# Where the scores' two waits stand among TensorE's column-strip sums in the attention stacks

## What is computed

```
for i in range(6):
    x = attn_layer(shift_tokens(x), Wqkv[i], q_scale[i], k_scale[i], Wo[i]) + x
    x = ffn_layer(shift_tokens(x), ln_g[i], ln_b[i], W1[i], b1[i], W2[i], b2[i]) + x

# attn_layer, 16 heads of 64, window 32
q, k, v = split(x @ Wqkv)
q = l2norm(q) * qs;  k = l2norm(k) * ksc
q, k = rotary(q), rotary(k)
out = softmax(mask(8 * q @ k.T)) @ v        # a query sees 64 keys: its window and the one before
return out @ Wo
```

## Time and profile before

| | us |
|---|---|
| median of three runs | 4347.09 |
| fastest and slowest of them | 4330.38, 4347.27 |
| the profiled execution | 4352.9 |
| its span, first to last instruction | 4351.2 |
| TensorE busy (matmuls) | 4027.8, 93% of the span |
| VectorE busy | 3345.6, 77% |
| ScalarE busy | 3100.0, 71% |
| GpSimd busy | 1798.7, 41% |

### The profile page before, as it was taken

The page is one execution under the profiler, slowest core; times in us unless marked ns, Lnnn a source line. Parts: engine busy times, 40 slices in busy tenths (PEclk is TensorE's granted clock), DMA queues, the critical chain, the costliest instruction groups (busy, mean ns, idle before and its releaser), DMA issues. The chain is left out here.

```text
span 4351.2 us, 113662 instructions
## 1 busy us (share of the span) xinstructions
PE 4027.8 (93%) x43857; PEld 2388.8 (55%) x43857; DVE 3345.6 (77%) x4981; ACT 3100.0 (71%) x7032; POOL 1798.7 (41%) x1071
## 2 busy tenths in 40 slices
PE   7997999999999999999967689999999999999998
PEld 3443555555555555555536545555555555555554
DVE  5774888888888888888735478888888888888885
ACT  3555777777777777777762267777777778777776
POOL 3111444444444444444404534444444444444442
PEclk7997999999999999999986589999999999999999
DMA  2212444444443443444300044444434444444342
GB/s 44 31 21 70 95 111 102 99 101 101 105 111 90 111 107 90 111 99 103 84 10 3 3 107 109 101 97 109 110 87 115 102 100 100 102 105 111 92 100 52
DMA packets 232520, 380.78 MB, mean 88 GB/s; under 512 B 59364, under 2 KB 122336, under 8 KB 231688
## 3 DMA queue, kind: packets, MB, share of 16 engines
q1 hardware_dynamic: 231560, 372.20, 36.9%
q10 hardware_dynamic: 384, 0.79, 0.1%
HBM read 39.22 MB, written 1.05 MB: 9 GB/s over the span
## 5 line engine op out<-in xcount | busy, mean ns | idle before, releaser
L835 POOL TENSOR_TENSOR b_prob<-b_prob,b_rinv 128x768 f32<-128x768 f32 x384 | 564.3, 1469 | 1778.3 <-DVE b_rinv L1281 1778.3
L841 POOL TENSOR_TENSOR b_prc<-b_prc,b_sws 128x1024 f32<-128x1024 f32 x384 | 907.7, 2364 | 72.2 <-DMA b_sws<-b_prs 72.2
L1143 ACT ACTIVATE b_prob<-ps,b_nmx 128x96 f32<-128x96 f32 x3072 | 749.0, 363 | 0.0
L885 PEld LDWEIGHTS ps<-ident,b_prob 128*128 128x128 f32 x3072 | 367.9, 140 | 406.5 <-ACT b_pT L1079 232.8
L1216 DVE SCALAR_TENSOR_TENSOR b_prc<-ps,b_qks,b_rot 128x512 f32<-128x512 f32 x768 | 571.1, 744 | 14.0 <-ACT b_sq L1104 13.3
L1218 DVE SCALAR_TENSOR_TENSOR b_prs<-ps,b_qks,b_rot 128x512 f32<-128x512 f32 x768 | 570.1, 742 | 0.0
L885 PE MATMUL ps<-ident,b_prob 128*128 128x128 f32 x3072 | 513.0, 281 | 46.5 <-DVE b_kr L1264 37.1
L1262 DVE TENSOR_TENSOR b_prc<-b_prc,ps 128x512 f32<-128x512 f32 x384 | 263.6, 686 | 369.9 <-PE ps L950 288.3
L1079 ACT ACTIVATE b_pT<-ps 128x512 f32<-128x512 f32 x724 | 435.5, 601 | 154.1 <-PE ps L885 151.1
L987 PE MATMUL ps<-b_wqkv,b_xs 128*128 128x256 f32 x1536 | 435.0, 406 | 2.2 <-DVE b_prs L1218 2.2
L938 PE MATMUL ps<-b_xs,b_wqkv 128*128 128x512 f32 x768 | 408.9, 614 | 23.3 <-issue 10.0
(11 more groups left out here) (293 smaller groups left out, 7218.0 us busy)
## 6 DMA issues: line engine op xcount, KB each, us to landing
b_sws<-b_prs SPq DMA_DIRECT2D x1536, 128.0 KB, 2.3
b_vs<-b_va SPq DMA_DIRECT2D x384, 256.0 KB, 3.8
b_wqkv<-in_L_ffn_Wqkv SPq DMA_DIRECT2D x96, 192.0 KB, 3.6
b_xs<-y SPq DMA_DIRECT2D x126, 128.0 KB, 2.3
b_wo<-in_L_ffn_Wo SPq DMA_DIRECT2D x96, 64.0 KB, 3.1
b_xs<-y SPq DMA_DIRECT2D x42, 127.8 KB, 2.4
b_rot<-in_rot SPq DMA_DIRECT2D x2, 2048.0 KB, 7.8
b_w<-in_L_ffn_W SPq DMA_DIRECT2D x24, 170.5 KB
```

The lines of the kernel that those rows point to most:

```text
L835: pool.tensor_tensor(prob[:, r, :, P - KEYS:P], prob[:, r, :, P - KEYS:P], rinv[:, r % 2, :].rearrange("p (b a) -> p b a", a=1).broadcast_ ...
L841: pool.tensor_tensor(prc[:, r, :, :], prc[:, r, :, :], sws[:, r % 2, :, :], ALU.add)\
L885: t = pe.transpose(bank[6][:, i * P:(i + 1) * P], prob[:, kd, 4 * e + 2 * h + m, :], ident[:, :])
L1143: g = act.activation(prob[:, kb, i, P - KEYS:P], wide[0][:, e * CH + m * KEYS:e * CH + (m + 1) * KEYS], ACT.Exp, bias=nmx[:, kb % 2, i:i + 1])
```

## The change

The function `strips` gets an argument `ahead`. Where it is set (and there is a unit b), `scores_ready` is called ahead of the fourth strip, inside the group. In odd slots in which the strips directly follow the second `turn` (all odd ones but those with `before == 5`), `turn` no longer gets b, so its last transposition waits for nothing of its own, and the call of `scores_ready` ahead of the masks, which only slots without a unit d had, falls away there. Even slots and the slots with `before == 5` keep their order. The number of matmuls and of waits stays the same, and nothing changes on the other engines.

```
-                def strips(U, b, pe=pe):
+                def strips(U, b, ahead, pe=pe):
                     pe.wait_ge(S["sqk_done"], ONE + U + 1)
                     if b:
                         pe.wait_ge(S["qn_done"], ONE + um(b)[0] + 1)
                     for s in range(4):
+                        if s == 3 and b and ahead:
+                            scores_ready(um(b)[0])
                         m = pe.matmul(bank[2][32 * s:32 * s + 32, :], head_of[:, :], sq[:, s, :],
                                       start=True, stop=True, skip_group_check=True)
                     m.then_inc(S["ss_mm"], 1)
@@
                     if d and before != 5:
-                        turn(UD, kd, 1, b)
+                        turn(UD, kd, 1, None if a and j % 2 else b)
                     if a and j % 2 and before != 5:
-                        strips(U, b)
+                        strips(U, b, True)
                     if b:
-                        if not d:
+                        if not d and not (a and j % 2):
                             scores_ready(UB)
                         mask(kb)
@@
                     if a and j % 2 and before == 5:
-                        strips(U, b)
+                        strips(U, b, False)
```

## The result

The changed kernel takes 4351.55 us (median of 20 runs, 4344.37 to 4371.22), the kernel before on the same chip 4343.36 (20 runs). One of the latter 20, of 5764.32 us, was a slow one and is left out of the ratio. The ratio is 1.0027, with a 95% interval of 1.0014 to 1.0039: 11.7 us longer, 6 to 17. That is also how far apart the means lie (4355.2 and 4343.5); the medians are 8.2 us apart, for seven of the 20 executions of the changed kernel took over 4360 us and none of the other 19 did. The forecast was +3.4 us, so the sign and the case were right and the size was too small. The profiled execution of after took 4345.22 us, with a span of 4343.2.

What follows compares the result with a forecast made beforehand. The prediction took TensorE, busy in 93% of the span, as the bound. Steady slots +6.3 us and late slots -2.9 gave net +3.4, hence 4350.5 us, range 4334 to 4365.

Steps and rivals of the forecast that it cites:

- the sign and the case: Whole kernel: slower, because line 875's wait record shows between third and fourth strip; +3.4 us, chance 0.6.
- The steady slots: 90 feed-forward odd slots: the record ahead of the fourth strip delays the masks 0.07 us each, +6.3 us.
- The second case of the forecast, the hidden record: Fourth strip: the record runs unseen while the strips wait for the square of k; 4343.0 us, chance 0.27.
- the rule that the forecast cites: TensorE's queue: a control instruction runs while engine instructions stand queued, so the record would cost nothing.
- The slower rival: Strip group: the late fourth strip starts behind the others' first round, 0.4 us per group; +45 us, 4392, chance 0.06.
- The register step: Loop layers: a register step beside the moved waits costs 0.1 us in 64 slots, +6 us more, 4356.9; upper bound.
- The last transposition: Its wait for the keys goes; in 97 slots it comes some 0.03 us earlier for nothing, value 0.
- The late slots: 47 odd slots with late keys: strips load earlier; gain 0 in 26, kept in 21, together -2.9 us.
- the 21 slots j = 3 and 19: Late-key slots where earlier strips were to keep their gain: 0.12 us in 15, 0.25 in four; together -2.9 us.
- the other 26 late slots: Late-key slots j = 1, 7, 9, 11, 13, 15 and 17, where GpSimd comes last: earlier strips gain 0.

Runs made afterwards that it cites:

- both waits at the masks: Against the kernel before: both waits moved behind the four strips, ahead of the first mask, behind a long-met wait for `take_set`; 4338.50 us, 0.9993.
- feed-forward slots alone: The change made only in slots j = 5, 7, 11, 13, 21, 23, 27 and 29, against the kernel before; 4345.77 us, 1.0005.
- waits at the first strip: The changed kernel with its two moved waits ahead of the first strip instead of the fourth, against the kernel before; 4341.47 us, 0.9994.
- small loads without the change: The kernel before with W1 and W2 loads cut to 8 columns in all layers but the first; 4338.89 us, 0.9991.
- the other slots alone: The change made only in odd slots j = 1, 3, 17, 19 and the first layer's 9 and 15, against the kernel before; 4343.40 us, 1.0003.
- small loads with the change: The changed kernel with W1 and W2 loads cut to 8 columns in all layers but the first, against the kernel before; 4352.07 us, 1.0034.
- four waits behind the strips: The kernel before with four more long-met waits behind the last strip, ahead of the first mask; 4349.96 us, 1.0018.
- The two parts alone: The change made only in feed-forward slots, then only in the other odd slots, each against the kernel before; 4345.77 us, 1.0005, and 4343.40 us, 1.0003.
- the short GpSimd and the change: The changed kernel with GpSimd's L835 cut to one of eight blocks, against the kernel before; 4311.87 us, 0.9932.
- both kernels with four waits: The kernel before with four more long-met waits, ahead of the fourth strip (4364.61 us, 1.0053) or behind the last strip (4349.96 us, 1.0018).
- four waits inside the group: The kernel before with four more long-met waits ahead of the fourth strip, which made two records; 4364.61 us, 1.0053.

## Why the forecast was right in kind and short in size

**The steady slots** (90 x 0.07 = +6.3 us): right. The fourth strip loads 0.089 us after the first, where the forecast had 0.095. The masks stand 0.070 us later as a mean of 88 slots, the stretches of 80 slots 4.6 us longer (means of the two traces of each kernel, 2104.7 and 2100.1), 0.06 each. The mechanism holds in each of its parts. The record runs only once the wait ahead of it is met: the order of waits decides, since with the pair ahead of the unmet wait the cost is gone. It is passed on in full: one record 0.07, two 0.18. The second case of the forecast, the hidden record, is refuted by the same rows. So is, for this place, the rule that the forecast cites from the Trainium skill, "Advanced Engine Details and Errata", section "Sequencer and Instruction Queues".

Two more slots change than the forecast counted, j = 3 of the two first layers, which have no unit d; their masks come 0.07 us later too, 0.1 us together.

**The slower rival** (the fourth strip falls out of the group, +45 us): refuted. A strip that loads 0.089 us after the first, even one at 0.195, is still taken along; the masks come at 1.07 and 1.17 and not at 1.4.

**The register step** in the loop's layers (+6 us): the steady slots inside the loop have the same 1.066 as those outside, so it costs nothing here.

**The last transposition** (value 0): right; in the steady slots it comes 0.03 us earlier (0.109 after the third instead of 0.141), and the kernel with both waits at the masks, which has only this, is no different from before there.

**The late slots** (-2.9 us): wrong, and this is the step that failed: "In the 21 slots j = 3 and 19 `rsp` stands behind the output projection's sum, which TensorE feeds, and the feed-forward slots follow: there the gain stays". The first half is as it was put: the strips came 0.18 us earlier, and `rsp` began 0.11 earlier. But its start is not its end. It lies beside GpSimd's L841, and what it gains at the start it loses in duration: 0.80, 0.92 and 0.97 us for starts 2.11, 1.99 and 1.93 us after L841's. The rows for this were at hand in the forecast, in which `rsp` takes 2.17 us instead of 0.74 beside L841, and were used for the other 26 late slots only. For the twelve slots j = 19 the term is 0. For the nine slots j = 3 no run shows the gain either, but none rules it out: the pairs j = 3 and 4 of all twelve layers take 221.6 and 219.2 us in the two traces of before and 223.8 and 222.0 after, and they scatter by more than the gain would be.

**What was not in the sum at all**: the slots j = 19 and 20 of the second stack. The pairs over twelve layers have a mean of 215.9 us in six traces that have no record between those strips (the kernel before twice, feed-forward slots alone, waits at the first strip, waits at the masks, small loads without the change) and 219.5 in the four with one (the changed kernel twice, the other slots alone, small loads with the change): +3.6 us. But the kernel with four waits behind the strips has no record there either and takes 220.8, by a late copy instead of a late swap. (In the second trace of the changed kernel late copies have a part too, 0.8 us in the first stack.) So the +3.6 came with the change, and is not the record's own cost. The forecast asked what was late next in each slot, and not whether a transfer stood at an edge one slot further.

Together: 6.3 + 0 + 3.6 = 9.9 us. Measured are 11.7 by the ratio, with an interval of 6 to 17, 8.2 by the medians, and 7.1 for both stacks by the traces. So no further cause is needed, though the measurements do not exclude one. That the forecast's time, 4350.5 us, lies within 1.1 of the median after is luck: it started from the median of three executions, 4347.09, and the median of 20 is 3.7 lower. The two parts alone measured 1.0005 and 1.0003, 0.0008 in sum against 0.0027 for the whole; each of these is uncertain by 0.0011 or so, so the split rests on the traces and not on the times.

**Why the swap lands late in the second stack.** No run was made for this, but the traces on record narrow it down. Besides the queue of the kernel's transfers (q1) the profile lists a queue q8 of kind "instruction", whose packets of 16 KB take 0.9 to 1.8 us. In the 2.06 us from the issue of the late transfer on (2966.66 to 2968.72, the case shown above), the DMA view of after has, among others (queue: packets, MB, share; then the issue with its KB and us to landing):

```profile
q8 instruction: 1, 0.02, 4.6%
b_sws<-b_prs SPq DMA_DIRECT2D x1, 128.0 KB, 4.1
```

In the same stretch behind the same transfer in the second stack's third layer of before (3274.76 to 3276.83), where it is issued as late, there is no packet of q8:

```profile
b_sws<-b_prs SPq DMA_DIRECT2D x1, 128.0 KB, 2.4
```

All 18 slots j = 19 with late keys (4, 5, 3 and 5 in the four traces above, one with the short GpSimd and the change) look like the first: the transfer takes 3.6 to 4.8 us, and in 16 of them a q8 packet of 16 KB starts 1.29 to 1.38 us behind its issue (1.79 and 2.19 in the other two). In 48 other slots j = 19 it is issued as late, with the packet 1.85 to 2.70 us behind it, and the keys are on time. Five of these are in the first trace of before, and there too `rsp` starts ahead of L841. So the turned order, with the later issue, is not enough to make the keys late. The late copies `b_xs<-y` of the second stack (3.5 to 4.2 us instead of 2.3, in both kernels with four waits) have such a packet 1.28 to 2.00 us behind their issue. And over all 14 traces, where a landing is known, 1421 of 4919 swaps and copies that had such a packet during their flight took over 3.3 us, of 17401 that had none 2.

**What stays open**: that the packet holds up the transfer is read from this coincidence; no run moved the packets alone. And why they fall on the swap or the copy in the second stack of some kernels and not of others was not traced. The W1 and W2 loads are not the cause by their size.

## What to carry to other kernels

A wait that is surely met costs nothing only if it stands ahead of the wait that ends last, or behind a group long enough to cover it. Between products that run side by side behind an unmet wait it costs its whole time, here 0.07 us for the first record and 0.11 for the second in each slot. Before an earlier start is booked as a gain, ask what the step runs beside: here `rsp` started earlier beside GpSimd's sum and ended no earlier. And a difference of some microseconds can come from one transfer that lands 2 us late for another reason: look at the slots that got longer before you put it down to the edit's own cost.

## What the runs showed of the hardware

TensorE's sequencer held a wait record until the wait ahead of it was met, then let the next load through 0.07 us later than without it, and 0.11 later still with a second record. One record can hold two waits, for one semaphore (four waits inside the group) or for two (both waits at the masks). Of four products on column strips, the last may load 0.195 us after the first and is still taken along; the next group moves by 0.07 and 0.18 us, not by a round. Of VectorE's `rsp` and GpSimd's L841 the one that starts 0.06 to 0.08 us earlier keeps its length while the other is held up by 0.5 to 2.1 us. And a swap or copy took over 3.3 us to land in 2 of 17401 cases without a 16 KB packet of the instruction queue in its flight, and in 1421 of 4919 with one.
